# First attention on one Trainium2 core: row sums and output product as bfloat16 products of high and low parts

## The reference, cut to what matters

```python
theta_x = jnp.einsum('ld,bdt->btl', theta_w, input2) + theta_b
phi_x = jnp.einsum('ld,bdt->blt', phi_w, input1) + phi_b[:, None]
scores = jnp.einsum('btl,bls->bts', theta_x, phi_x)
p = jax.nn.softmax(scores, axis=-1)
g_x = jnp.einsum('ld,bdt->btl', g_w, input1) + g_b
t_x = jnp.einsum('bts,bsl->blt', p, g_x)
mu = jnp.mean(t_x, axis=(1, 2), keepdims=True)
var = jnp.var(t_x, axis=(1, 2), keepdims=True)
h = (t_x - mu) * jax.lax.rsqrt(var + LN_EPS) * ln_gamma + ln_beta
h = jax.nn.relu(h)
w_t = jnp.einsum('ol,blt->bot', out_w, h) + out_b[None, :, None]
return w_t + input2
```

## Time and profile before

| | us |
|---|---|
| median of 3 runs | 773.13 |
| lowest, highest | 772.34, 775.3 |
| the profiled execution | 767.05 |
| its span | 765.3 |
| mean granted clock of TensorE | 0.993 |

### The profile page before, as it was taken

The page is one execution under the profiler, slowest core; times in us unless marked ns, Lnnn a source line. Parts: engine busy times, 40 slices in busy tenths (PEclk is TensorE's granted clock), DMA queues, the critical chain, the costliest instruction groups (busy, mean ns, idle before and its releaser), DMA issues.

```text
span 765.3 us, 14396 instructions
## 1 busy us (share of the span) xinstructions
PE 721.5 (94%) x4285; PEld 303.1 (40%) x4285; DVE 571.4 (75%) x1108; ACT 406.0 (53%) x757; POOL 356.5 (47%) x349
## 2 busy tenths in 40 slices
PE   5999999899999999989999999999998998999995
PEld 2444444344444444311232222222223554555553
DVE  4688888898685958678888898998967765554553
ACT  2544444564654647257877776777687443222221
POOL 4565544312102031256567656776755464354433
PEclk9999999999999999989999999999999999999998
DMA  9999890006537197333433344444464796999975
GB/s 308 385 132 221 266 344 1 1 1 208 199 131 276 54 361 254 109 98 95 114 84 111 101 101 137 136 117 128 155 208 102 153 182 116 130 155 150 136 112 69
DMA packets 114182, 117.51 MB, mean 154 GB/s; under 512 B 54840, under 2 KB 78264, under 8 KB 113856
## 3 DMA queue, kind: packets, MB, share of 16 engines
q1 hardware_dynamic: 103008, 94.48, 43.8%
q0 software_dynamic: 10384, 22.02, 16.6%
q10 hardware_dynamic: 720, 0.13, 0.1%
HBM read 43.61 MB, written 59.56 MB: 135 GB/s over the span
## 4 chain that ended last, share of the span: by engine, by line
PE 24%; DMA 14%; issue 8%; DVE 4%; POOL 3%; SPq 2%; POOLq 1%; ACT 1%; DVEq 0%; ACTq 0%
PE l_b L1511 7%; DMA out<-t_room,t_tag 7%; PE l_pv L1522 6%; PE l_sm L1530 6%; DMA out<-l_pvs,t_tag 4%; PE l_a L1452 2%; DMA out<-l_sums,t_tag 2%; SPq L1015 2%; PE l_b L1465 1%; DVE h_negm L1744 1%; DVE l_negm L1744 1%; POOLq L1203 1%; DMA l_stack<-h_wide 1%; PE l_b L1502 1%; POOL l_pvs L2079 1%
## 5 line engine op out<-in xcount | busy, mean ns | idle before, releaser
L1652 ACT ACTIVATE t_room<-l_b 128x512 f32<-128x512 f32 x256 | 139.0, 594 | 37.0 <-PE l_b L1511 36.1
L1744 DVE TENSOR_REDUCE l_negm<-l_a 128x2 f32<-128x1024 f32 x64 | 75.2, 1219 | 8.3 <-PE l_a L1452 8.2
L1130 PE MATMUL l_a<-w1h,h_stack 128*128 x312 | 76.3, 313 | 3.6 <-DVE l_stack L1183 2.0
L1159 ACT ACTIVATE l_stack<-l_stack 128x352 f32<-128x352 f32 x39 | 19.4, 496 | 105.9 <-DVE l_stack L1183 105.9
L1744 DVE TENSOR_REDUCE h_negm<-l_a 128x2 f32<-128x1024 f32 x56 | 65.9, 1219 | 8.4 <-PE l_a L1452 8.3
L1522 PE MATMUL l_pv<-t_room,l_vt 128*32 128x512 f32 x512 | 69.1, 612 | 0.1
L1530 PE MATMUL l_sm<-t_room,ones_f 128*32 128x512 f32 x512 | 68.2, 604 | 0.0
L825 PE MATMUL ps_st<-f_xt,wg 128*128 128x512 fp8e4 x256 | 65.7, 379 | 1.1 <-ACT f_xt L729 0.8
L825 PE MATMUL ps_r<-f_xt,wg 128*128 128x512 fp8e4 x256 | 65.7, 379 | 0.0
L974 POOL TENSOR_TENSOR X<-X,f_y 128x512 f32<-128x512 f32 x16 | 20.1, 1258 | 79.8 <-ACT f_y L875 79.8
L1213 POOL DMA_INDIRECT out<-t_room,t_tag x20 | 31.6, 1579 | 40.1 <-DVE t_room L1198 14.2
(11 more groups left out here) (296 smaller groups left out, 1544.9 us busy)
## 6 DMA issues: line engine op xcount, KB each, us to landing
slots_x<-empty SPq DMA_DIRECT2D x8, 2376.0 KB, 11.2
slots_x<-empty SPq DMA_DIRECT2D x7, 2112.0 KB, 16.5
h_stack<-h_wide SPq DMA_DIRECT2D x96, 64.0 KB
l_stack<-h_wide SPq DMA_DIRECT2D x96, 64.0 KB
f_stage<-in_w SPq DMA_DIRECT2D x8, 704.0 KB, 7.2
f_stage<-in_w SPq DMA_DIRECT2D x8, 512.0 KB
h_wide<-in_ctx SPq DMA_DIRECT2D x16, 256.0 KB, 3.2
l_vt<-in_ctx_t SPq DMA_DIRECT2D x16, 256.0 KB, 3.0
```

The source lines that it names most:

```text
L1130: mm = pe.matmul(self.HP[i % 2][:, 0:self.H], T.xt[i % T.AHEAD][:, xp * self.FC + f, :], self.w1[wp][:, bass.ds(e, 1), f * self.H:(f + 1) ...
L1652: act.activation(weights_at(u, c, h)[:, :], B[t % 2][:, :], ACT.Exp, scale=SCALE).then_inc(b_ok, 1)
L1744: dve.tensor_reduce(negm[u % 2][:, 2 * half:2 * half + 2, j], A[half][:, :, :], AX.X, ALU.max, negate=True)\
```

## The change

A float product on TensorE becomes two or three bfloat16 products, of a high part (rounded to bfloat16) and a low part (the rest). For the sums, ScalarE makes the high part of psa and GpSimd the low part (they lie in psb, which is free by then), and TensorE multiplies both with ones. For the output product, ScalarE's relu writes the high part of h as bfloat16, a second relu writes it as float (hf), GpSimd takes the difference; the weights are split once in step 0; TensorE makes weight high and low by h high, and weight high by h low. The output product of batch 7 moves from m = 8 to m = 9 in the network.

```diff
+        psp = psb[:, :].bitcast(BF16).rearrange("p (n d) -> p n d", n=2)
...
         def sums_of(pe, i):
-            pe.wait_ge(row_sum, i)
-            pe.matmul(SM[:, :], ones_f[:, :], psa[:, :], start=True, stop=True).then_inc(sum_ps, 1)
+            pe.wait_ge(psl_ok, i)
+            pe.matmul(SM[:, :], ones_b[:, :], psp[:, 0, :], start=True, stop=False)
+            pe.matmul(SM[:, :], ones_b[:, :], psp[:, 1, :], start=False, stop=True).then_inc(sum_ps, 1)
...
         def out_of(pe, n, banks):
-            pe.wait_ge(wo_in, 16)
+            pe.wait_ge(wop_ok, 2)
             pe.wait_ge(h_ok, n)
+            wait(pe, res_ok, 2 * n - 2)
             for o in range(2):
-                wait(pe, res_ok, 2 * n - 2)
-                pe.matmul(banks[o][:, :], wo[:, o * P:(o + 1) * P], h[:, :], start=True, stop=True).then_inc(out_ps, 1)
+                for wp in range(2):
+                    pe.matmul(banks[o][:, :], wop[:, wp, o * P:(o + 1) * P], h[:, 0, :], start=wp == 0, stop=False)
+            pe.wait_ge(hl_ok, n)
+            for o in range(2):
+                pe.matmul(banks[o][:, :], wop[:, 0, o * P:(o + 1) * P], h[:, 1, :], start=False, stop=True).then_inc(out_ps, 1)
...
-            if m == 8:
+            if m == 9:
                 pe.wait_ge(G.xt_ok, 2)
                 out_of(pe, B - 1, A)
...
-            act.activation(h[:, :], txb[:, :], ACT.Relu).then_inc(h_ok, 1)
+            act.activation(h[:, 0, :], txb[:, :], ACT.Relu).then_inc(h_ok, 1)
+            wait(act, hl_ok, n - 1)
+            act.activation(hf[:, :], txb[:, :], ACT.Relu).then_inc(hf_ok, 1)
+
+        def high_sums(act, i):
+            act.wait_ge(row_sum, i)
+            act.activation(psp[:, 0, :], psa[:, :], ACT.Copy).then_inc(psh_ok, 1)
...
                 act.activation(phi_h[:, :], R[1][:, :], ACT.Identity, bias=bias[:, 1:2]).then_inc(high_ok, 1)
+                if back:
+                    high_sums(act, i)
...
             G.spread(act, 0)
+            high_sums(act, B)
             act.wait_ge(sum_ps, B)
...
+        def low_sums(pool, i):
+            pool.wait_ge(psh_ok, i)
+            pool.tensor_tensor(psp[:, 1, :], psa[:, :], psp[:, 0, :], ALU.subtract).then_inc(psl_ok, 1)
+
+        def low_hidden(pool, n):
+            pool.wait_ge(hf_ok, n)
+            pool.tensor_tensor(h[:, 1, :], hf[:, :], h[:, 0, :], ALU.subtract).then_inc(hl_ok, 1)
...
                 pool.tensor_tensor(xi, xi, ctxb[par][:, :, :], ALU.add).then_inc(ctx_added, 1)
+                if back:
+                    low_sums(pool, i)
+                else:
+                    pool.wait_ge(wo_in, 16)
+                    pool.tensor_copy(wop[:, 0, :], wo[:, :]).then_inc(wop_ok, 1)
+                    pool.wait_ge(wop_ok, 1)
+                    pool.tensor_tensor(wop[:, 1, :], wo[:, :], wop[:, 0, :], ALU.subtract).then_inc(wop_ok, 1)
...
                 else:
                     G.power(pool, 0)
+                if back2:
+                    low_hidden(pool, i - 1)
...
             pool.tensor_tensor(psa[:, :], psa[:, :], psb[:, :], ALU.add).then_inc(row_sum, 1)
-
-        def last_gpsimd(pool, n):
-            root_of(pool, n)
+            low_sums(pool, B)
+
+        def last_gpsimd(pool, part):
+            if part == 0:
+                root_of(pool, B - 1)
+            if part == 1:
+                low_hidden(pool, B - 1)
+                root_of(pool, B)
+                low_hidden(pool, B)
```

More of the change, by code:

```diff
@@ L135, in latent_attention @@
         beta = kept("beta", [L, D])
-        tx, txb, h = kept("tx", [L, D]), kept("txb", [L, D]), kept("h", [L, D])
+        tx, txb, h = kept("tx", [L, D]), kept("txb", [L, D]), kept("h", [L, 2, D], BF16)
+        hf = kept("hf", [L, D])
+        wop = kept("wop", [L, 2, S], BF16)
         tst = kept("tst", [L, 6])
@@ L161, in latent_attention @@
         t1_ok, bet_ok, h_ok, out_ps, res_ok = (sem(n) for n in ("t1", "bet", "h", "outps", "res"))
+        wop_ok, hf_ok, hl_ok, psh_ok, psl_ok = (sem(n) for n in ("wop", "hf", "hl", "psh", "psl"))
         def steps(eng, step):
@@ L353, in relu @@
             wait(act, out_ps, 2 * n - 2)
-            act.activation(h[:, :], txb[:, :], ACT.Relu).then_inc(h_ok, 1)
+            act.activation(h[:, 0, :], txb[:, :], ACT.Relu).then_inc(h_ok, 1)
[4 more added lines that the diff above has]
+            act.activation(psp[:, 0, :], psa[:, :], ACT.Copy).then_inc(psh_ok, 1)
         def biased(act, i):
             act.wait_ge(tx_ok, i)
-            wait(act, h_ok, i - 1)
+            wait(act, hf_ok, i - 1)
             act.activation(txb[:, :], tx[:, :], ACT.Identity, bias=bias[:, 2:3]).then_inc(txb_ok, 1)
@@ L574, in last_vector @@
                 spread_of(dve, B)
-            if m == 9:
+            if m == 10:
                 added(dve, B - 1, A)
@@ L957, in group @@
                 if g == 0:
-                    last.gpsimd(pool, last.batches - 1)
+                    last.gpsimd(pool, 0)
                 if more:
@@ L961, in group @@
                 if g == 0:
-                    last.gpsimd(pool, last.batches)
+                    last.gpsimd(pool, 1)
                 if not more:
```

## The result

| | before | after |
|---|---|---|
| median, 6 runs each | 773.12 us | 780.26 us |
| lowest, highest | 772.34, 775.3 | 778.83, 781.97 |
| the profiled execution, its span | 767.05, 765.3 | 781.19, 779.4 |

The ratio is 1.0089 (95% interval 1.0071 to 1.0107): 6.9 us slower (7.1 by the medians), where 7.2 were forecast. The two profiled executions differ by twice that, 14.1 us. So I took a second profile of the kernel before (774.53 us, span 772.8) and read the change against both. The stretches are cut at starts that the timelines show: L437 of steps 2 and 7 (L455 in the changed kernel), the network's first product (L825, now L866), and its last (L841, now L882).

What follows compares the result with a forecast made beforehand. A loop through TensorE's sums, ScalarE and VectorE was taken to bound attention steps, TensorE the gated network. The terms 0 + 2.1 + 2.97 + 3.0 - 0.86 = +7.2 us gave 780.3 us, range 775 to 783.

Steps and rivals of the forecast that it cites:

- What bounds a step: First attention: a loop through TensorE's sums product, ScalarE and VectorE sets the step, 16.57 us; the output product is off it.
- The port in the steps, +2.1: Steps 2 to 6: low_hidden on GpSimd holds VectorE's L456, and L615 holds L508; +0.42 us per step, +2.1 for five.
- Rival 2: Clock falls, but low_hidden comes after L456 and doesn't block it; steps at about 0, +5.1 us, 778.2 us; chance 27%.
- ends before theta is late: Attention steps: the output product's wait for its low part ends before theta is delayed; its gain is worth nothing there.
- Step 1, 0: Step 1, without relu: low_sums holds L529, 0.47 us lost against 0.43 gained by the sums; taken as 0.
- The seam, +2.97: Attention to gated network: slower normalizations (+0.9) and the last sums waiting for their parts delay the first network product 2.97 us.
- The clock, +3.0: Around the seam's transposes: two TensorE pauses over 3 us halve the clock, so the network starts slow; 3.0 us lost.
- taking 6 us of it: Gated network's start: assumed 6 us of the network run at half speed, losing 3.0 us.
- The network, -0.86: Gated network: the last two output products stand between its matmuls, and their shorter time counts fully; -0.86 us.
- TensorE never idles: Gated network: TensorE was taken as always busy between the matmuls, so the last two output products gain 0.86 us.
- The sum: Whole kernel: 0 + 2.1 + 2.97 + 3.0 - 0.86 = +7.2 us, forecast 780.3 us; chance 40%.

## Why the prediction was right, point by point

- **What bounds a step.** Right. The sums, which are on the loop, give 0.37 us a step when alone (16.40 for 16.77). The output product, which isn't, has the same gain on TensorE and no step shows it: in the changed kernel TensorE only stands still for longer, 0.37, 0.49 and 0.34 us in the step in which it stood 0.33. Its gain can't be run without its helpers, so this is read from the waits and not from a time.
- **The port in the steps, +2.1.** Right in kind: 1.6 to 1.7 came. L456 waits (0.71 to 0.78 us more, 0.87 forecast), GpSimd's addition ends at 122.80 (forecast 122.83), the next L508 begins at 122.32 (122.39) and is held a little longer (1.57 us for 1.46). The term is 0.4 us too high, since the sums' product gave 0.52 us, not 0.43: two passes of float needed 0.96 us to the first score, which I had in hand and put at 2 x 0.43.
- **Rival 2** took the steps at 0 if low_hidden came later. The run with low_hidden later does not bear this out: the five steps still lose 0.86 us, since TensorE's wait takes over. In the prediction's words, its wait "ends before theta is late" only as long as low_hidden is early.
- **Step 1, 0.** Right: L547, which was L529, takes 1.05 us (0.17 before), and what the sums gain pays for it: from the first maximum of step 1 to the L437 of step 2 it is 20.66 us, 20.76 and 20.78 in the two profiles of before.
- **The seam, +2.97.** Right, and 0.5 too low. +0.92 for the normalizations (forecast 0.9), the rest by the wait for low_sums; 3.46 in all, since the two sums passes themselves went at half clock (0.81 us to the network for 0.43).
- **The clock, +3.0.** Right that it falls, too high in size. The eight passes of the network's first two blocks took 3.41 us for 1.72; with what is left in the third, about 1.8, and 0.38 at the seam: 2.2 us, and 2.3 by the filled pauses. The mis-sized step is "taking 6 us of it": 3.6 us of the network were at half clock. I had let the low clock begin with the network; it began 3.2 us ahead of it (147.70 to 150.94), where TensorE mostly stood. Two pauses were not needed either: one of 3.05 us was enough in the run with the last sums in float. And I had read the first profile's pause of 2.18 us as harmless. It is not, always: the second profile has 0.51 over 3.5 us behind a pause of 2.19, and the run with the sums in the steps has half clock behind one of 2.35. Part of the cost (0.68 us in the network) is so paid by the kernel before too, in some of its executions.
- **The network, -0.86.** This step failed, though its bounds held: next to nothing was left of the gain. With full clock at its start the network takes 176.45 and 176.51 us with both output products in float (the sums in the steps with the pause filled, the first profile of before), and 176.32, 176.45 and 176.49 with both in bfloat16 (the filled pauses, the last sums in float, the output product alone). The products were shorter by 0.4 us each, but "TensorE never idles" did not hold: VectorE lost 0.9 us to the last but one low_hidden (L953 takes 1.34 us once, for 0.43), its additions to x were moved one place later with the product (from m = 9 to m = 10 in the code), and TensorE waited for VectorE at two places, both ahead of the last low_hidden, at 189.30 us:

```profile
178.99 0.38 PE L229 MATMUL ps_sm<-w1h,mean_f 128*128 128x1 f32 x2 [0.23 <-DVE w1h L450]
...
187.17 0.39 PE L882 MATMUL ps_pv<-wl,f_h 128*128 128x512 fp8e4 x1 [0.19 <-DVE f_h L953]
```

  How much of this is due to the held L953 and how much to the later place of the additions is not shown.
- **The sum** was close (7.2 forecast, 6.9 by the times, 6.6 between the changed kernel's profile and the second of before) because the misses have both signs: steps -0.4, clock -0.8, a further -0.7 because that profile of before pays for half clock too, network +0.8, seam without the clock +0.1, and 0.5 in the rest. Without the first profile the rest takes 448.7 to 451.1 us from profile to profile, so 0.5 is nothing to explain. That clock and network nearly cancel is luck.

## What to carry to other kernels

Work that is taken from TensorE is worth something where the next event waits for TensorE, and nothing where a wait stands behind it: find the loop first, then cut. The helpers that make operands for cheaper products are not free on idle engines: each has a place in its engine's order, can hold back an instruction of VectorE that runs beside it, and lengthens the chain at the seams, where nothing runs beside it. A pause of 3 us on TensorE cost twice here, once for itself and once in the slower products behind it, and filling it with products of no use took the second cost away. And one profile is one execution: the first one of the kernel before lacked a pause of 8 us, far from the change, that all the others had.

## What the runs showed of the hardware

- Of a VectorE and a GpSimd instruction that both read their operands from SBUF in the ways met here, the one that starts later takes longer by about the rest of the earlier, less 0.15 us: L474 started 0.23 us behind low_hidden, which went on for 0.93 us, and took 0.78 us more (the difference is 0.14 to 0.15 us in all five steps); without the overlap it took 0.69 in every step. The rule of the Trainium skill, page "SBUF — State Buffer", section "Who interferes with whom", agrees: who issues first keeps the pair of ports. The runs show the waits; that a port is behind them is what the page says.
- The four normalizations from float to fp8 (one SBUF tensor each) take 4.04 us beside three GpSimd additions, 4.95 to 5.09 beside three and a subtraction of 1.16 us: the fourth instruction of GpSimd adds 0.9 to 1.05 us, most of its own length.
- The granted clock at the seam, by TensorE's pause before the transposes: it stayed at 1.00 through pauses of 2.18 us (before, first profile) and 2.34 (sums alone, up to a second pause of 3.80), fell behind 2.19 (before, second profile) and 2.35 (sums in the steps), and fell in every kernel with an unfilled pause of 3.05: ahead of the transposes in three, in the changed kernel 1 us into the second pause. Filled with 26 bfloat16 products of no use, or with ten where the pause was 2.3 us, it stayed at 1.00.
- With the pause of 2.55 us at the start of the head attention the clock fell to half, for 6.8 to 10.2 us in all ten profiles.
